# Causal zeros by a select on GpSimd, and another order of steps in three attention stages

## The reference, cut to what matters

```python
K, Q, V = (to_heads(K), to_heads(Q), to_heads(V))
Q = _rope(Q, freqs)
K = _rope(K, freqs)
scores = jnp.einsum('bhqd,bhkd->bhqk', Q, K) / sqrt(d)
causal = jnp.triu(jnp.ones((S, S), dtype=bool), k=1)
scores = jnp.where(causal, -jnp.inf, scores)
probs = jax.nn.softmax(scores, axis=-1)
heads = jnp.einsum('bhqk,bhkd->bhqd', probs, V)
```

## Time and profile before

| | us |
|---|---|
| median of 3 runs | 3789.82 |
| lowest, highest | 3786.21, 3791.73 |
| the profiled execution | 3788.22 |
| its span, first to last instruction | 3786.4 |
| causal stage, about | 50 to 510 |
| cross stage, about | 555 to 905 |
| band stage, about | 2525 to 2940 |

### The profile page before, as it was taken

How to read it: one execution, slowest core, us unless ns; L and a number is a source line. 1 busy time by engine, 2 the same in 40 slices (tenths; PEclk the granted TensorE clock), 3 DMA queues, 4 the chain that set the end, 5 groups by cost and what they waited for, 6 DMA issues and landing times. The chain is left out here.

```text
span 3786.4 us, 93267 instructions
## 1 busy us (share of the span) xinstructions
PE 3288.4 (87%) x33694; PEld 2790.3 (74%) x33695; DVE 2719.1 (72%) x10688; ACT 1203.2 (32%) x3140; POOL 2068.0 (55%) x2392
## 2 busy tenths in 40 slices
PE   6999957786599999999999999978888897699998
PEld 4777735554488888888888888855564687699998
DVE  6666634554999999999999999948887554533333
ACT  1443435552222222222222222225664221122221
POOL 4444335551677777777777777858885000233333
PEclk8999978997799999999999999989999896799999
DMA  5444434443000000000000000034453115466665
GB/s 152 110 108 110 109 83 116 123 113 122 1 2 2 2 2 2 2 2 2 2 2 2 2 2 2 2 91 124 125 130 74 34 33 160 123 181 183 182 182 136
DMA packets 256114, 277.90 MB, mean 73 GB/s; under 512 B 44001, under 2 KB 200673, under 8 KB 255201
## 3 DMA queue, kind: packets, MB, share of 16 engines
q1 hardware_dynamic: 242081, 253.69, 23.5%
q0 software_dynamic: 13632, 18.91, 3.3%
HBM read 187.63 MB, written 72.29 MB: 69 GB/s over the span
## 5 line engine op out<-in xcount | busy, mean ns | idle before, releaser
L1190 POOL TENSOR_TENSOR peer_hot_v<-peer_hot_e,peer_parts 80x512 bf16<-80x512 bf16 x768 | 990.9, 1316 | 320.9 <-DVE peer_hot_e L1233 311.7
L1009 PE MATMUL peer_ps_u<-peer_up,peer_g 128*128 128x256 f32 x2048 | 534.3, 408 | 0.6 <-DVE x_all L1331 0.6
L990 PEld LDWEIGHTS peer_ps_h<-peer_xnT,peer_down 128*128 128x128 f32 x4096 | 512.7, 197 | 15.7 <-DMA peer_down<-in_peer_down 0.9
L990 PE MATMUL peer_ps_h<-peer_xnT,peer_down 128*128 128x128 f32 x4096 | 512.3, 280 | 0.6 <-DMA peer_down<-in_peer_down 0.6
L1000 PE MATMUL peer_ps_w<-peer_hot_v,peer_hot_u 80*128 80x32 bf16 x12288 | 347.3, 177 | 145.4 <-DVE peer_g L1245 97.5
L1000 PEld LDWEIGHTS peer_ps_w<-peer_hot_v,peer_hot_u 80*128 80x128 bf16 x12288 | 337.0, 97 | 167.3 <-issue 92.1
L1009 PEld LDWEIGHTS peer_ps_u<-peer_up,peer_g 128*128 128x128 f32 x2048 | 393.1, 202 | 53.5 <-issue 1.0
L1087 ACT ACTIVATE peer_g<-peer_ps_h 128x512 f32<-128x512 f32 x256 | 152.9, 597 | 840.5 <-PE peer_ps_h L990 840.2
L1237 DVE TENSOR_TENSOR peer_hot_u<-peer_count,peer_uvT 80x2048 bf16<-80x2048 bf16 x256 | 349.4, 1365 | 0.0
L2072 POOL DMA_INDIRECT out<-moe_y,moe_target x71 | 112.6, 1585 | 312.6 <-DVE moe_y L2203 309.6
L2007 PE MATMUL moe_ps_t<-moe_xgT,moe_w 128*128 128x128 f32 x2272 | 267.3, 276 | 0.0
(11 more groups left out here) (362 smaller groups left out, 7073.9 us busy)
## 6 DMA issues: line engine op xcount, KB each, us to landing
moe_w<-in_moe_w SPq DMA_DIRECT2D x142, 512.0 KB
causal_qs<-causal_qscratch SPq DMA_DIRECT2D x32, 384.0 KB, 3.9
cross_qs<-cross_qscratch SPq DMA_DIRECT2D x32, 384.0 KB, 3.6
band_qs<-band_qscratch SPq DMA_DIRECT2D x32, 384.0 KB, 4.1
moe_w<-in_moe_w SPq DMA_DIRECT2D x8, 1024.0 KB, 11.7
causal_qscratch<-causal_part SPq DMA_DIRECT2D x32, 192.0 KB, 2.6
causal_kscratch<-causal_part SPq DMA_DIRECT2D x32, 192.0 KB, 2.0
causal_ks<-causal_kscratch SPq DMA_DIRECT2D x32, 192.0 KB, 4.2
```

The source lines that it names most:

```text
L990: mm = nc.tensor.matmul(ps_h[:, n % 2, k * P:(k + 1) * P], down[:, c, 4 * n + k, :], xnT[:, par, c, :], start=(c == 0), stop=(c == DC - 1))
L1009: mm = nc.tensor.matmul(ps_u[:], g[:, par, v, :], up[:, v, :], start=(v == 0), stop=(v == EV - 1))
L1190: ins = nc.gpsimd.tensor_tensor(hot_v[0:SEL, n % RING, part], hot_e[0:SEL, n % RING], w, ALU.mult)
```

## The change

Three things are changed in `attention_stage`.

1. The mask of the causal stage. In `head` nothing is added any more; the exponentials are taken unmasked, and GpSimd sets those above the diagonal to zero afterwards with one `affine_select` over the two diagonal blocks of a head (128 partitions x 2 x 128), in `factor`. `weigh` waits for this instead of for ACT. In `find` the two added products become one of 256 columns.
2. The order. In all three stages find(b + 1, s) stands right behind head(b, s) and factor(b, s - 1), ahead of the other entries of the step. The last projection goes from step 11 to step 10. In the causal stage `moments` and `norm` go from steps 3 and 4 to 12 and 14.
3. The rotation on DVE is cut in two: `project` does the two products, and `project_end`, one step later, the two sums.

```diff
-        PROJECT, OUT, VALUES, STACK = (2, 5, 8, 11), 13, 15, 8
-        WEIGH, SUMS, NORMALISE, MOMENTS, NORM = 6, 4, 7, 3, 4
+        PROJECT, OUT, VALUES, STACK = (2, 5, 8, 10), 13, 15, 8
+        WEIGH, SUMS, NORMALISE = 6, 4, 7
+        MOMENTS, NORM = (12, 14) if rope else (3, 4)
...
                 if s > 0:
                     e.factor(b, par, s - 1)
+                if there(b + 1):
+                    e.find(b + 1, 1 - par, s)
...
                         e.project(b + 2, par, PROJECT.index(s))
+                    if s - 1 in PROJECT:
+                        e.project_end(b + 2, par, PROJECT.index(s - 1))
...
                     if s == VALUES:
                         e.values(b + 1, 1 - par)
-                    e.find(b + 1, 1 - par, s)
...
                         mm = nc.tensor.matmul(ps_1[:, h % 2, c0:c0 + n], qs[0:ROWS, par, h, q * P:(q + 1) * P],
-                                              ks[0:ROWS, par, h, 0:n], start=True, stop=not rope)
-                        if rope:
-
-                            mm = nc.tensor.matmul(ps_1[:, h % 2, c0 + q * P:c0 + (q + 1) * P], ident16[:], mask[:, 0, :],
-                                                  start=False, stop=True)
+                                              ks[0:ROWS, par, h, 0:n], start=(not rope or q == 0), stop=not rope)
+                    if rope:
+                        diagonal = ps_1[:, h % 2, :].rearrange("p (n k) -> p n k", k=P)[:, 0:3:2, :]
+                        mm = nc.tensor.matmul(diagonal, ident16[:], mask[:].unsqueeze(1).broadcast_to((P, TT, P)),
+                                              start=False, stop=True)
...
                         mm = nc.tensor.matmul(ps_2[0:KN, h % 2, c0:c0 + n], ks[0:ROWS + 3, par, h, k * KN:(k + 1) * KN],
-                                              qs[0:ROWS + 3, par, h, qfrom[k]:S], start=True, stop=not rope)
-                        if rope:
-                            mm = nc.tensor.matmul(ps_2[:, h % 2, c0:c0 + P], ident16[:], mask[:, 1, :],
-                                                  start=False, stop=True)
+                                              qs[0:ROWS + 3, par, h, qfrom[k]:S], start=True, stop=True)
...
+                    elif rope:
+                        pe.wait_ge(b_ready[0], HEADS * b + 4 * j + 4)
...
                 def factor(self, b, par, h):
+                    if rope:
+                        pool.wait_ge(p_ready, HEADS * b + h + 1)
+                        e = probT[:, h, :].rearrange("p (n q) -> p n q", q=P)[:, 0:KT * TT - 1:2, :]
+                        nc.gpsimd.affine_select(e, e, [[0, KT], [1, P]], ALU.is_ge, 0.0, base=0,
+                                                channel_multiplier=-1).then_inc(b_ready[0], 1)
+                        return
...
-                    steps.link(nc.vector.tensor_tensor(rot[:, j % 2, 1, :], bank[:, S:2 * S], tab[sn][:], ALU.mult))
-
+                    nc.vector.tensor_tensor(rot[:, j % 2, 1, :], bank[:, S:2 * S], tab[sn][:], ALU.mult).then_inc(rotated, 1)
+
+                def project_end(self, b, par, j):
+                    if not rope:
+                        return
+                    qk, c = JOBS[j]
+                    dve.wait_ge(rotated, NJ * b + j + 1)
                     wait(dve, split_ready, NJ * b + j - 1)
                     wait(dve, parts_out[c], OUTS * b)
```

More of the change, by code:

```diff
@@ L172, in attention_stage @@
             ident16 = sb("ident16", [P, P], BF16)
-            mask = sb("mask", [P, 2, P], BF16)
-            maskf = sb("maskf", [P, 2, P])
+            mask = sb("mask", [P, P], BF16)
+            maskf = sb("maskf", [P, P])
             rot = sb("rot", [P, 2, 2, S])
@@ L228, in attention_stage @@
         split_ready = sem("split_ready")
+        rotated = sem("rotated")
         parts_out = [sem(f"parts_out{c}") for c in range(DC)]
@@ L319, in program @@
                 e.project(0, 0, j)
+                e.project_end(0, 0, j)
             e.stack(0, 0, 0)
@@ L327, in program @@
                 e.project(1, 1, j)
+                e.project_end(1, 1, j)
             e.stack(1, 1, 0)
@@ L350, in project, with project_end @@
             def project(self, b, par, j): pass
+            def project_end(self, b, par, j): pass
             def stack(self, b, par, c): pass
@@ L381, in _ @@
                     sp.dma_start(tab[n][:], d[f"{n}"]).then_inc(weights, 16)
-                sp.dma_start(maskf[:], chunks(d["mask"])).then_inc(weights, 16)
+                sp.dma_start(maskf[:], d["mask"]).then_inc(weights, 16)
             else:
@@ L2235, in _constants @@
     far = np.full((P, P), -1e30, f)
-    c["mask"] = np.concatenate([np.triu(far, 1), np.tril(far, -1)])
+    c["mask"] = np.triu(far, 1)
     row, col = np.arange(P)[:, None], np.arange(P)[None, :]
```

## The result

| | before | after |
|---|---|---|
| median of 4 runs, us | 3788.8 | 3810.21 |
| lowest, highest | 3786.21, 3791.73 | 3805.88, 3812.55 |
| span of the profiled execution | 3786.4 | 3806.4 |
| one causal macro | 28.53 | 27.16 |
| one band macro | 24.57 | 26.58 |

The ratio of after to before is 1.0055, interval 1.0038 to 1.0072: slower by 21 us, half a per cent; the interval leaves out 1. The forecast was 3797, the range 3765 to 3836, and slower had the largest of the three chances.

What follows compares the result with a forecast made beforehand. PE bounds causal, three nearly full engines make order decide band, and PE waits for DMA in cross; -4 - 3 + 15 - 1 = +7 on 3788.22 gave 3795, forecast as a median of 3797 us, range 3765 to 3836.

Steps and rivals of the forecast that it cites:

- six selects: Causal macro: two selects before weigh(0), four before weigh(2); 0.06 us a macro for each 0.01 us of select price.
- part 1: Causal stage: the shorter mask products save PE 0.114 us a head, 1.8 us in each macro.
- part 3: Causal macro followed step by step: 28.2 us against 28.53, so -4 us over 14 macros.
- the walk: Part 3's timing of a causal macro: PE waits for POOL 1.2 us before weigh(0), 2.2 before weigh(2).
- part 2: Price of one select on POOL, bounded by neighbouring operations between 0.43 and 1.25 us, taken as 0.60.
- The last causal macros (-3): Last two causal macros, without projections: PE's 1.8 us once and little in the tail, where ACT sets the pace; -3 us.
- part 4: Band: project(3)'s split delays factor 10 and weigh(2); +1.1 us a macro, +15 over 14, -1 for the last two.
- Cross (0): Cross stage: an earlier find doesn't shorten the ring through POOL and DRAM; 0 us, with 2 us to either side.
- A: Rival, cheap select: 0.43 us each, 1.0 us less a causal macro, total 3783; chance 0.20.
- B: Rival, PE stays the bound: selects and band's split find gaps on POOL; 3756, or 3765; chance 0.13.
- C: Rival, dear select: from 0.655 us up the causal macro lengthens; 3822 at 0.9, 3851 at 1.25; chance 0.17.
- D: Rival, the clock: PE's idle stretches in causal and band lower it, +25 us over 28 macros, 3822; chance 0.08.

Runs made afterwards that it cites:

- experiment 3: The changed kernel with the select touching only one element of each block, so the zeros above the diagonal are not made; 3792.83 us (one run).
- experiment 4: The changed kernel with each head's select made as two instructions of 128 columns, same result; 3820.06 us (one run).
- experiment 9: The changed kernel with the last projection back in step 11 in cross and band, and POOL's causal splits moved behind the selects; 3744.84 us, ratio 0.9888.
- experiment 1: The changed kernel with POOL's split of project(3) in band put back behind the factor of head 10, other engines unchanged; 3783.99 us, ratio 0.9979.
- experiment 2: The changed kernel with the last projection back in step 11 in cross and band, on all engines; 3779.51 us, ratio 0.9967.
- experiment 11: The kernel of experiment 9 with `out` of the causal stage in step 14 instead of 13; 3775.93 us, ratio 0.9959.

## Why the prediction was right or wrong

- **PE's saving and the six selects (parts 1 and 3): right as a mechanism.** Both waits stand where the walk put them. With the measured 0.41 in place of 0.60 the walk gives weigh(0) at 10.2 - 2 x 0.19 = 9.8 and a macro of 28.2 - 6 x 0.19 = 27.06; measured are 296.18 - 286.39 = 9.8 and 27.16. Experiments 3 and 4 measured the slope that the walk had worked out, 6 for each select: 5.8 and 6.5.
- **The select's price (part 2): mis-sized.** 0.41 lies just below the lower bound, 0.43, that came from the MEMSET and CAST rows; the value taken went by the two-input TENSOR_TENSOR, and it was 0.19 too high. In the causal stage this is the term that carried the miss: 6 x 0.19 x 12 = 13.7 us over the first twelve distances, which were off by 11.7; the walk with the right price is 0.1 a macro too short, and gives back 1.2 of it. The Trainium skill (GPSIMD Engine Reference, Performance pitfalls for Q7 kernels) has the two figures from which the prediction worked out its estimate of 0.42 to 0.63 us; the measured 0.41 agrees with the lower one, for an unrolled loop.
- **What the earlier find and the cut rotation take away (part 3): right in kind, too small.** The forecast had PE's 1.8 us and these waits go nearly all into two new waits for POOL, and costed the order and the mask together. The order alone is worth 1.5 us a macro (27.00), the mask nothing on top of it as the splits stand; in the old order the mask costs 0.65. The 1.8 us of PE's work pay only when the splits are out of the way too (experiment 9).
- **The last causal macros (-3): wrong sign, +4.1.** The working took PE's saving there and assumed ACT's pace. The window from 432 to 501 is 69 us long with PE busy for 52.77 and the clock at 0.88, against 67 with 55.77 and 0.95 before. With the nearly free select the last three distances together are 0.4 us longer than before, but with two selects 2.3 and with the order alone 2.6, so the selects' price doesn't explain it by itself. How much of the +4.1 is the clock was not separated.
- **Band, the place and the queue (part 4): right.** turn_max(1) starts on POOL at 1.6 (forecast 1.7) with no wait on PE, weigh(0) at 8.94 (9.0), the queue from the split of project(2) to weigh(2) is 2691.12 - 2683.06 = 8.06 long (8.15), the rest 3.18 (3.2). Experiments 1 and 2 take the split of project(3) out from ahead of the factor and get 25.03 and 24.54. PE's wait ahead of weigh(2) is 1.49 us, not some 2.5, since PE itself comes later than the walk had it.
- **Band, the start of that queue: mis-sized.** The split of project(2) was to start at 14.4 and starts at 2683.06 - 2667.72 = 15.3. These 0.9 us in each macro make it 26.58 instead of 25.7: +2.0 us, outside the bounds of +0.65 to +1.3 that the prediction gave for this sum. They arise between weigh(0), which is on time, and project(2): in PE's band rows the two finds and the normalise product between them wait for DVE, 0.20, 0.47 and 0.40 us, 1.07 in all, where PE waits for nothing in the kernel before. The same three waits stand in experiment 2, where the split is back in its old place. So they come with the early find: at this place it costs 0.5 us (15.3 against 14.8 before), where the prediction counted 0.4 us of a gain as left. A part is that DVE's own instructions are slower there, 1.25, 1.01 and 1.13 against 0.97, 0.83 and 0.97 us, 0.6 in all; see the last section.
- **Band, the count of 14 macros: right.** From the first head to the first `onT`, with one macro that has a projection, it is +3.2, the eleven full distances give +21.6, the twelfth +1.3: 26.1 us, against 15 forecast. The last three distances are 1.9 us shorter than before (forecast -1).
- **Cross (0): +3.3, not settled.** Among kernels with the late find the stage is 304.2 us (before), 307.2 and 308.0 long, among ten with the early one 307.5 to 313.5. So the early find may cost a few us there, but the spread within each group is as large as the difference of their means, and the granted clock over the stage is 0.90 in both kernels.
- **The joints: +7.3 against 0.** 5.1 of them lie between the last cross and the first band `onT`. Of these 3.2 belong to the band stage, as said above: the stretch from its first head is 40.1 to 41.0 us in the four kernels that keep the new split in band, and 36.7 to 37.6 in the nine others. The peer stage is 2.4 us longer, and its length varies by 4.9 us between kernels with the same code there. The other joints were not explained.
- **The rivals.** A had the select's price nearly right, and its causal gain came; its total of 3783 did not, since the band stage lost more. B fell: POOL's queue is what weigh waits for, in both stages. C fell with the price. D did not happen in the middle of the causal and band stages, where the granted clock is 1.00 with waits of 1.16 and 1.49 us in each macro. The Trainium skill (TensorE: Matmul & The Clock Gate, Part 1) says that idle time lowers it. The end of the causal stage agrees, 0.88 where PE is idle for a quarter of the time, and the runs show no clear border: experiment 11 has 0.94 with a longest wait of 1.33 us.
- **The arithmetic.** Two sums are a little off. B's second figure, 3765, comes out at 3767 or 3768 by its own shares. The halves as stated give 0.31 for "same" and 0.46 for "slower", not 0.34 and 0.43.

The total was near partly by luck. The first twelve causal distances came out 12 us better than the forecast; the last causal macros came out 7 us worse, band with its first stretch 10, cross 3, and the other joints 4.

## What to carry to other kernels

Work taken from a full engine and given to one with room is paid for in the order of the receiving queue, not in its busy time: here 16 selects of 0.41 us fitted easily, and still cost 1.8 us a macro until the splits that nobody was waiting for went behind them. When a step moves, look on each engine for what it has passed: one split ahead of one factor was worth 1.5 of 26.6 us. And try an order without the work that came with it: in the changed kernel the order carried the whole causal gain, and the cheaper mask paid only after the splits had moved as well.

## What the runs showed of the hardware

Some of DVE's instructions slow down while POOL works. DVE's pair of factors in the band stage, two inputs of 130 columns each, timeline of the changed kernel:

```profile
2700.52 1.25 DVE L803 TENSOR_TENSOR band_probT<-band_probT,band_band 128x130 f32<-128x130 f32 x2
...
2703.16 1.01 DVE L742 TENSOR_SCALAR band_xn<-x_all,mean,rstd 128x256 f32<-128x256 f32 x2
...
2705.56 1.13 DVE L803 TENSOR_TENSOR band_probT<-band_probT,band_band 128x130 f32<-128x130 f32 x2
...
2681.83 0.48 DVE L803 TENSOR_TENSOR band_probT<-band_probT,band_band 128x130 f32<-128x130 f32 x2
```

and the first three in the kernel before:

```profile
2692.09 0.97 DVE L785 TENSOR_TENSOR band_probT<-band_probT,band_band 128x130 f32<-128x130 f32 x2
2693.86 0.83 DVE L729 TENSOR_SCALAR band_xn<-x_all,mean,rstd 128x256 f32<-128x256 f32 x2
...
2696.62 0.97 DVE L785 TENSOR_TENSOR band_probT<-band_probT,band_band 128x130 f32<-128x130 f32 x2
```

The pair takes 0.48 us while POOL waits for ACT (2680.44 to 2683.06) and 1.13 to 1.25 while POOL is in its row without a gap; in the kernel before it took 0.97 beside the same POOL operations. In the causal stage of the changed kernel the second sum of a rotation takes 0.41 to 0.42 us each of the 45 times that POOL does nothing beside it, and 0.88 to 0.90 each of the 19 times that POOL works during a part of it. Not every instruction minds: the reduction of a band find from its bank takes 0.68 us (median) with POOL idle and with POOL busy, and the first sum of a rotation mostly 0.41 either way. So the price of some instructions on DVE depends on what POOL runs beside them, up to 2.6 times, and a new order changes it. That they contend follows from when it happens; no run here took POOL away to measure it by itself.

A select on GpSimd costs 0.178 us for 1 x 2 elements, 0.292 for 128 x 128 and 0.406 for 128 x 256 (medians): about 0.18 us, and 0.9 ns for each element of a partition.

The third is the clock of experiment 11: 0.94 in eleven causal macros on end, where every other kernel has 1.00 in the first eleven distances.
